# Four of sixteen token transposes move from TensorE to the DMA queues and VectorE

## What is computed

```python
xn = _layernorm(x)
# attention branch: 16 heads, decayed causal scores, layer norm, silu gate, wo
logits = xf @ router_w.T + router_b
top_vals, top_idx = jax.lax.top_k(logits, 4)
rw = softmax(top_vals) * 1.8
routed = sum over the 4 experts: rw * (silu(xf @ gate.T) * (xf @ up.T)) @ down.T
shared = silu(xf @ shared_gate.T) * (xf @ shared_up.T) @ shared_down.T
x = x + attention(xn) + routed + shared
```

## Time and profile before

| | |
|---|---|
| time, median of 3 runs (lowest to highest) | 200.17 us (200.09 to 200.4) |
| time of the profiled execution | 200.26 us |
| its span, first to last instruction | 198.4 us |
| granted TensorE clock | 1.0 of full speed |
| busy: PE, weight loads, DVE, ACT, POOL | 190.0, 142.7, 117.5, 96.7, 111.8 us |

### The profile page before, as it was taken

How to read it: one execution, slowest core, us unless ns; L and a number is a source line. 1 busy time by engine, 2 the same in 40 slices (tenths; PEclk the granted TensorE clock), 3 DMA queues, 4 the chain that set the end, 5 groups by cost and what they waited for, 6 DMA issues and landing times.

```text
span 198.4 us, 4872 instructions
## 1 busy us (share of the span) xinstructions
PE 190.0 (96%) x1734; PEld 142.7 (72%) x1734; DVE 117.5 (59%) x360; ACT 96.7 (49%) x242; POOL 111.8 (56%) x156
## 2 busy tenths in 40 slices
PE   8998999999998899899999999999999999999994
PEld 2665756778565667698888678887867877687863
DVE  3478789898897766765632532433342144426894
ACT  3146248555889342653238647734934941123500
POOL 4133057525979468777777677777877743730000
PEclk9999999999999999999999999999999999999999
DMA  4994999998000029999975634324433335229963
GB/s 133 316 374 159 332 403 421 446 444 378 7 0 3 5 56 380 384 358 366 366 288 149 223 106 140 97 90 138 123 104 98 115 91 220 79 82 292 373 262 132
DMA packets 15000, 42.33 MB, mean 213 GB/s; under 512 B 2677, under 2 KB 6138, under 8 KB 14336
## 3 DMA queue, kind: packets, MB, share of 16 engines
q1 hardware_dynamic: 11376, 33.03, 45.5%
q0 software_dynamic: 3456, 8.92, 13.3%
q10 hardware_dynamic: 144, 0.07, 0.2%
HBM read 34.66 MB, written 7.86 MB: 214 GB/s over the span
## 4 chain that ended last, share of the span: by engine, by line
PE 73%; DMA 7%; DVE 7%; issue 4%; POOL 4%; ACT 3%; SPq 0%; ACTq 0%; POOLq 0%; DVEq 0%
PE bank L1575 20%; PE bank L1591 8%; PE bank L1783 5%; PE bank L1589 5%; DMA xg_mem<-xn_rows,codes 4%; PE bank L1440 4%; PE bank L1450 3%; PE bank L1553 3%; DMA w_mem<-w_qkvg_dram 3%; PE bank L1541 3%; PE bank L1612 3%; PE bank L1515 3%; DVE w_mem L1105 2%; PE bank L1465 2%; PE bank L1817 2%
## 5 line engine op out<-in xcount | busy, mean ns | idle before, releaser
L1575 PE MATMUL bank<-xb_mem,w_mem 128*128 128x128 f32 x384 | 47.7, 276 | 0.1
L1575 PEld LDWEIGHTS bank<-xb_mem,w_mem 128*128 128x128 f32 x384 | 45.4, 192 | 0.8 <-issue 0.3
L838 POOL DMA_INDIRECT y_rows<-y_mem,codes x36 | 36.2, 1007 | 16.8 <-issue 9.4
L830 POOL DMA_INDIRECT xg_mem<-xn_rows,codes x36 | 35.4, 984 | 13.0 <-issue 9.7
L1160 DVE TENSOR_TENSOR h_mem<-h_mem,bank 128x128 f32<-128x128 f32 x32 | 9.2, 287 | 42.2 <-ACT h_mem L641 41.9
L1105 DVE TENSOR_TENSOR w_mem<-bank,w_mem 128x512 f32<-128x512 f32 x32 | 20.1, 682 | 2.9 <-PE bank L1465 2.8
L640 ACT ACTIVATE h_mem<-bank 128x128 f32<-128x128 f32 x32 | 8.9, 277 | 23.5 <-PE bank L1575 23.1
L1168 DVE COPY y_mem<-bank 128x256 f32<-128x256 f32 x36 | 15.0, 424 | 7.3 <-PE bank L1591 4.5
L653 ACT COPY w_mem<-w_mem 128x1024 f32 x16 | 16.0, 1042 | 3.2 <-PE bank L1630 2.2
L1591 PE MATMUL bank<-w_mem,h_mem 128*128 128x256 f32 x60 | 17.0, 405 | 0.0
L1440 PE MATMUL bank<-w_mem 128*128 128x128 f32 x128 | 15.9, 278 | 0.2 <-DMA w_mem<-w_qkvg_dram 0.2
(11 more groups left out here) (168 smaller groups left out, 320.7 us busy)
## 6 DMA issues: line engine op xcount, KB each, us to landing
w_mem<-w_exp_dram SPq DMA_DIRECT2D x3, 3456.0 KB, 21.6
w_mem<-w_late_dram SPq DMA_DIRECT2D x7, 1152.0 KB, 8.1
w_mem<-y_rows SPq DMA_DIRECT2D x8, 512.0 KB, 7.3
w_mem<-w_qkvg_dram SPq DMA_DIRECT2D x2, 512.0 KB, 6.3
w_mem<-decay_dram SPq DMA_DIRECT2D x2, 512.0 KB, 7.6
xn_rows<-w_mem SPq DMA_DIRECT2D x2, 512.0 KB, 3.4
xnt_rows<-w_mem SPq DMA_DIRECT2D x1, 1024.0 KB, 4.9
w_mem<-w_ovf_dram SPq DMA_DIRECT2D x16, 64.0 KB
```

What stands on the lines that cost most here:

```text
L830: nc.gpsimd.indirect_dma_start(xg[:, k % RING, :], None, xn_rows, bass.IndirectOffsetOnAxis(ap=codes[:, c, 0:1], axis=0),).then_inc(tok_in ...
L838: nc.gpsimd.indirect_dma_start(y_rows, bass.IndirectOffsetOnAxis(ap=codes[:, c, 1:2], axis=0), ysb[:, k % YRING, :], None, bounds_check=RO ...
L1575: last = nc.tensor.matmul(ps_gu[j][:, m * P:(m + 1) * P], w[:, o:o + P], xbT[:, p % 2, (2 * g + j) * P:(2 * g + j + 1) * P], start=(g == 0 ...
```

## The change

Blocks of the last four pairs (24 to 31; `FIRST = 12`) are transposed by DMA. The DMA transposes 2-byte elements, so the fp32 tokens are handled as two planes of 16-bit halves:

- In the head, ACT splits each of the eight tiles of `xn` into low halves and high halves (`split_tokens`) in `xg_mem`, four tiles at t = 1 and four at t = 2. SP stores them in device memory (`xn_halves`, 1 MB) ahead of the third batch of weights, and the writers of `pos_hot` on ACT and POOL wait for that store.
- For blocks 24 to 31, POOL gathers rows of `xn_halves`, SP issues a DMA transpose of the 128x512 block of 16-bit elements into a buffer `xp`, which lies in `ws_mem`, and DVE joins the planes into `xbT` (`take_tokens`). PE no longer transposes them and ACT no longer copies them.
- SP's order becomes: overflow groups 0 to 2, transposes of 24 to 27, overflow group 3, transposes of 28 to 31, then `ws_mem`, then `xnt_rows`. The load of `ws_mem` waits until DVE has joined all eight blocks.
- The semaphores `wo_in` and `tot_sb` become one each instead of one per block or tile, and PE waits for the loaded overflow weights in `down_overflow` instead of `gate_up_overflow`.

```diff
+FIRST = 12
-X_ORDER = [b for b in SEQ_X if b[0] == "O" or b[1] % 2 == 0]
+X_ORDER = [b for b in SEQ_X if b[0] == "O" or (b[1] % 2 == 0 and b[1] < 2 * FIRST)]
+        xg_halves = xg_mem[:, :].bitcast(U16).rearrange("p (a b) -> p a b", a=RING)
+        xn_staged = xg_mem[:, :].bitcast(U16).rearrange("p (t h d) -> p t h d", t=NT, h=2)
+        xn_split = xn.bitcast(U16).rearrange("p t (d h) -> p t h d", h=2)
+        xbT_halves = xb_mem[:, 0:4 * KT * P].bitcast(U16).rearrange("p (a g j n h) -> p a j h g n", a=2, g=KT, j=2, h=2)
+        xp = ws_mem[:, 0:4 * KT * P].bitcast(U16).rearrange("p (a j b n) -> p a j b n", a=2, j=2, n=P)
...
                 if p + BATCH_IN == EARLY:
+                    sp.wait_ge(st_halves, NT)
+                    sp.dma_start(xn_halves.rearrange("(p t) c -> p t c", p=P),
+                                 xn_staged.rearrange("p t h d -> p t (h d)")).then_inc(halves_out, 16)
                     sp.wait_ge(xnT_ps, len(HEAD))
...
-                if j == 0:
-                    sp.dma_start(ws_mem[:, :], w_shared).then_inc(ws_in, 16)
+            def transpose_block(n):
+
+                p, j, k = n // 2, n % 2, AT["P", n]
+                sp.wait_ge(tok_in[k % RING], 16 * (k // RING + 1))
+                if p >= FIRST + 2:
+                    sp.wait_ge(xt2_sb, 2 * (p - 2 - FIRST) + j + 1)
+                sp.dma_start_transpose(xp[:, p % 2, j], xg_halves[:, k % RING, :]).then_inc(tp_in[p % 2][j], 16)
+
+            for j in range(STATIC_O - 1):
+                group_in(j)
+            for n in range(2 * FIRST, 2 * FIRST + 4):
+                transpose_block(n)
+            group_in(STATIC_O - 1)
+            for n in range(2 * FIRST + 4, 2 * PAIRS):
+                transpose_block(n)
+            sp.wait_ge(xt2_sb, 2 * (PAIRS - FIRST))
+            sp.dma_start(ws_mem[:, :], w_shared).then_inc(ws_in, 16)
             sp.wait_ge(xt_ps, len(X_ORDER))
             sp.dma_start(xg_mem[:, :], xnt_rows).then_inc(xnt_in, 16)
...
+            def split_tokens(t):
+                act.wait_ge(xn_done, t + 1)
+                nc.scalar.copy(xn_staged[:, t], xn_split[:, t]).then_inc(st_halves, 1)
...
-                if 0 < s < PAIRS - 1:
+                if 0 < s < FIRST - 1:
                     take_pair_tokens(s + 1)
...
+            def take_tokens(n):
+
+                p, j = n // 2, n % 2
+                if j == 0:
+                    dve.wait_ge(gu_ps, 2 * (p - 1))
+                wait_transposed(dve, p, j)
+                nc.vector.tensor_copy(xbT_halves[:, p % 2, j], xp[:, p % 2, j].rearrange("p (h g) n -> p h g n", h=2)
+                                      ).then_inc(xt2_sb, 1)
...
             def expert_step(s):
                 if s < PAIRS:
                     multiply_unit(2 * s)
+                if FIRST <= s + 1 < PAIRS:
+                    take_tokens(2 * s + 2)
...
                 if 1 <= s and s != PAIRS - 1:
                     results(s - 1)
+                if FIRST <= s + 1 < PAIRS:
+                    take_tokens(2 * s + 3)
...
-                pe.wait_ge(xt_sb, X_AT["P", 2 * p] + 1)
+                if p < FIRST:
+                    pe.wait_ge(xt_sb, X_AT["P", 2 * p] + 1)
+                else:
+                    pe.wait_ge(xt2_sb, 2 * (p - FIRST) + j + 1)
...
-                if 0 < s < PAIRS - 1:
+                if 0 < s < FIRST - 1:
                     transpose_pair(s + 1)
```

More of the change, by code:

```diff
@@ L141, with build @@
 SENT = [sum(k % YRING == w for k in range(len(SEQ_Y))) for w in range(YRING)]
-X_ORDER = [b for b in SEQ_X if b[0] == "O" or b[1] % 2 == 0]
+X_ORDER = [b for b in SEQ_X if b[0] == "O" or (b[1] % 2 == 0 and b[1] < 2 * FIRST)]
 X_AT = {b: k for k, b in enumerate(X_ORDER)}
-def build(nc, x, consts, decay, w_router, w_qkvg, w_out, lnwb, rbias, w_exp, w_late, w_ovf2, w_shared, xn_rows, xnt_rows, y_rows, out):
+def build(nc, x, consts, decay, w_router, w_qkvg, w_out, lnwb, rbias, w_exp, w_late, w_ovf2, w_shared, xn_rows, xn_halves, xnt_rows, y_rows, out):
     with ExitStack() as ctx:
@@ L366, in build @@
         we_in = [sem(f"we_in{p}") for p in range(PAIRS)]
-        wo_in = [sem(f"wo_in{j}") for j in range(STATIC_O)]
+        wo_in = sem("wo_in")
         ones_sb = sem("ones_sb")
@@ L386, in build @@
         xt_sb = sem("xt_sb")
+        xt2_sb = sem("xt2_sb")
+        st_halves = sem("st_halves")
+        halves_out = sem("halves_out")
+        tp_in = [[sem(f"tp_in{a}{j}") for j in range(2)] for a in range(2)]
         gu_ps = sem("gu_ps")
@@ L418, in build @@
         diag_sb = sem("diag_sb")
-        tot_sb = [sem(f"tot_sb{i}") for i in range(NT - len(PE_TILES))]
+        tot_sb = sem("tot_sb")
         block = ctx.enter_context(nc.Block())
@@ L453, in down_bank, with whole_rows, wait_slot_read, wait_transposed @@
             return ps_dn[j][:, 0:D] if p < PAIRS - 1 else ps_sd[1][j][:, 0:D]
-        def x_done(k):
+        def whole_rows(k):
+            return SEQ_X[k][0] == "O" or SEQ_X[k][1] < 2 * FIRST
+        def wait_slot_read(eng, k):
             kind, n = SEQ_X[k]
-            return X_AT[kind, n - n % 2 if kind == "P" else n] + 1
+            if whole_rows(k):
+                eng.wait_ge(xt_ps, X_AT[kind, n - n % 2 if kind == "P" else n] + 1)
+            else:
+                wait_transposed(eng, n // 2, n % 2)
+        def wait_transposed(eng, p, j):
+            eng.wait_ge(tp_in[p % 2][j], 16 * ((p - FIRST) // 2 + 1))
         @block.sync
@@ L521, in _, with group_in @@
                     sp.wait_ge(y_ps, NT)
-                sp.wait_ge(we_in[p - 2 if p > EARLY else p - 1], 16)
-                late_pair_in(p)
-            for j in range(STATIC_O):
+                late_pair_in(sp, p)
+            def group_in(j):
                 experts = overflow_experts(SUBS * j)
                 if j == 0:
-                    sp.wait_ge(we_in[PAIRS - 1], 16)
                     sp.wait_ge(res_sb, NT)
@@ L551, in _ @@
                 else:
-                    sp.wait_ge(tot_sb[t], 1)
+                    sp.wait_ge(tot_sb, t + 1)
                 sp.dma_start(out_v[:, t, :], x_sb[:, t, :]).then_inc(out_done, 16)
@@ L710, in _ @@
                     take_features(3)
+                if t in (1, 2):
+                    split_tokens(4 * t - 4)
+                    split_tokens(4 * t - 3)
                 if t >= 2:
@@ L714, in _ @@
                 take_values_gate(t + 1)
+                if t in (1, 2):
+                    split_tokens(4 * t - 2)
+                    split_tokens(4 * t - 1)
                 hot_positions(t, "vg")
@@ L1317, in add_routed @@
                 if k == TOPK - 1 and n not in PE_TILES:
-                    ins.then_inc(tot_sb[n], 1)
+                    ins.then_inc(tot_sb, 1)
                 else:
@@ L1655, in down_overflow @@
                 pe.wait_ge(oht_sb, j + 1)
+                pe.wait_ge(wo_in, 16 * SUBS * (j + 1))
                 if j == 0:
@@ L1896 @@
     xn_rows = nc.dram_tensor("xn_rows", (TOK, D), F32, kind="Internal").ap()
+    xn_halves = nc.dram_tensor("xn_halves", (TOK, 2 * D), U16, kind="Internal").ap()
     xnt_rows = nc.dram_tensor("xnt_rows", (P, KT * TOK), F32, kind="Internal").ap()
     y_rows = nc.dram_tensor("y_rows", (ROWS, D), F32, kind="Internal").ap()
-    build(nc, *args, xn_rows, xnt_rows, y_rows, out)
+    build(nc, *args, xn_rows, xn_halves, xnt_rows, y_rows, out)
     r = run_bass_kernel_spmd(nc, [{n + "_dram": v for n, v in arrays.items()}], core_ids=[0])
```

19 lines of the change are left out of this document (12 added, 7 removed).

## The result

The changed kernel takes 203.06 us (median of 6 executions, 202.09 to 204.40), the kernel before beside it 200.25 (6 executions): a ratio of 1.0138 with a 95% interval of 1.0091 to 1.0185. It is slower by 2.8 us; 200.0 was predicted, and the range ended at 202.2.

The account below looks back on a forecast made before the run. PE was taken to bound the kernel. Terms -1.76 + 0.2 + 1.3 + 0.1, given as -0.17 on 200.26, made 200.1, less 0.09 for that execution lying over the median: 200.0 us, range 199.1 to 202.2.

Parts of the forecast that it names:

- PE's saving: Expert steps: four pairs' transposes leave PE, 0.44 us each on the chain, 1.76 us in all.
- the wait for the loads: Ahead of the shared expert: PE ready at 172.5, ws_mem and xnt_rows land at 173.8, so PE waits 1.3 us.
- the head: Start of the kernel: ACT's splits delay a copy PE needs; 0.1 us, bounds 0 and 0.3.
- the overflow weights: Step 13: ACT's copies of overflow block 3's weights end too late for PE; some 0.2 us lost.
- The four terms of the sum: Whole kernel: -1.76 PE's saving, +0.2 overflow weights, +1.3 wait for the loads, +0.1 head, given as -0.17 us.
- The transposes: DMA transposes of blocks 24 to 31: 4 us to landing, spacing up to 1.5, DVE waits 0.7 us, no cost.
- the two rules weighed: DMA transpose speed: one skill section gives 1309 ns per 128x128 square, the other says as fast as regular DMAs.
- late-halves rival: Head: store of halves lands at 48.3, holding ACT 1.7 us; up to 1.5 us more, 201.5; chance 0.10.
- The step that failed: Kernel's end: read-back from y_rows starts no later, its eight DMAs landing by about 192, nearly 4 us before the end.
- the rivals on record: Full gain, loads landing by 172.5 (198.7 us, chance 0.10); slow transposes (0.16); halves landing late (0.10).
- slow transposes: Blocks 28 to 31: DMA transposes hold each other up in one queue; 203.0 at 3.5 us spacing, chance 0.16.
- Every sign that was listed for the prediction being right: No line-1553 transposes after step 10; PE nearly gapless to 172.5, then 1.3 us gap ended by xnt_rows; ws_mem issued near 166.6.

Follow-up runs that it names:

- experiment 10: Kernel before plus only the head's splits, store of halves and waits on it, all transposes still on TensorE: 200.65 us, ratio 1.0013.
- Experiment 8: PE held before the shared expert by ACT copies. Kernel before: one 201.46 us, two 203.43, one plus late read-back 203.03; changed kernel without its two late loads: 200.93.
- experiment 6: Changed kernel, loads still late, with results of blocks 30 and 31 in memory of their own: 203.27 us, ratio 1.0146; profiled execution 200.67.
- experiment 3: Changed kernel with xnt_rows loaded once the last blocks in xg_mem are transposed, only ws_mem waiting for the last join: 199.57 us, ratio 0.9955.

## Why the prediction was wrong

**PE's saving and the wait for the loads** were right. PE is ready at 174.09 - 1.17 = 172.92 (172.5 forecast), `ws_mem` is issued at 166.78 (166.6), PE waits 1.17 us (1.3) and starts the shared expert where it did before (0.27 us earlier forecast). The 0.4 us of difference are 0.26 by which PE stood later at 139 us already, ahead of the first saved transposes (0.1 was put for the head; experiment 10 leaves 0 to 0.6), and 0.13 of PE's saving: the join of block 27 stood behind a copy that waited for a scatter, and PE lost 0.33 us there where 0.2 was put for the overflow weights. The four terms of the sum add up to -0.16, not -0.17.

**The transposes** were right, and better than their bounds: 3.3 us to landing where 4 was taken, 1.3 us apart, one wait of 0.8 on DVE where 0.7 was forecast, joins of 0.45 where 0.55 was. Of the two rules weighed, that of the Trainium skill in "VectorE: DVE Perf Modes", The three transpose paths, fell: its 1309 ns for each of four squares makes 5.2 us for a block, an estimate, and eight blocks landed in 3.1 to 3.8. They were not as fast as a plain transfer either: the 128 KB store took 1.8. The late-halves rival fell too: the store, issued at 38.78, needed 7.6 us by its line, to 46.4, and ACT's first write of `pos_hot` ran at 46.90 without a wait.

**The step that failed** is the sentence "The read-back from `y_rows` cannot start later for it: the last scatters follow `down_one`, which comes 1.5 us earlier, and its eight DMAs have landed by about 192, nearly 4 us before the end." Both halves are wrong. The last scatters follow `down_one` only if the slots of `y_mem` are free, and these come free when earlier scatters land; the moved load was put on top of just those scatters. The row for it was there: the copy at 167.46 that waited for a scatter in before, while `xnt_rows` was loading. I read it as a hold that the change takes away from step 13, and did not ask what the load would hold at its new place. And the slack of a transfer is not the time from the last landing to the end: the first additions stand ahead of `shared_hidden(3)` in DVE's list, so a read-back 1.85 us later moved the end by 0.7 in the kernel before, and one 1.66 us later by 1.3 in the changed kernel without loads.

**What was missing** is the clock. The prediction priced PE's wait at its length; in before no such pause exists there, and every term was taken from rows at full clock. Experiment 8 shows a pause of 1.49 us costing 3.1. The loss that the sum lacks has thus two parts: some 2.1 us in the executions at full clock (202.09 and 202.56 against 200.25), most of it by the late read-back (experiment 6 without it lost 0.4 at full clock), and some 1.4 more in the others. That a pause of PE is enough for the fall is shown by experiment 8, with and without the changed code; which of its two pauses it followed in the executions of the changed kernel that were not profiled is not known. Why pauses of like length were followed by a fall in some executions and not in others is open, as is the speed of the read-backs.

None of the rivals on record is what happened. The other side was given to slow transposes; the loss came from transfers that the change only moves. Every sign that was listed for the prediction being right was seen in the trace; none of them looked behind the start of the shared expert.

## What to carry to other kernels

When a transfer moves, list what else uses the DMA queues in the window that it moves into, and follow each of those to the buffer it frees and to the engine that waits for the buffer: a load that cost DVE 0.34 us at one place held a 128 KB scatter for 7 us at another, and DVE for 2.8. When a buffer is shared for a detour, as `ws_mem` was for the transposed halves, issue each load as soon as its own buffer is read for the last time: that alone, in experiment 3, turned +1.4% into -0.45%. A pause of an otherwise busy TensorE may cost twice its length, so a gap of a microsecond in the forecast deserves its own line in the sum and in the range.

## What the runs showed of the hardware

A scatter issued by POOL landed in 2.4 us when nothing else moved. In the changed kernel SP issued a 640 KB and a 1 MB load at 166.78 and 167.21, and three scatters issued at 167.18, 168.46 and 171.12 landed between 174.2 and 175.0 (after 7.06, 6.0 and 3.9 us), when the loads were through (174.0). With the 1 MB load cut into four, in shorter packets, scatters landed in 3.8 to 5.4 us, by the line of the scatters. The Trainium skill, "DMA: Bandwidth & Descriptors", Queues, rings and completion order, says that each DMA engine alternates between queue rows packet by packet. That shorter packets freed the scatters sooner goes with it; but packets and transfers were cut together, so no run here shows which of the two it was.

TensorE's granted clock fell to its 1.2 GHz level for a stretch of some 3 us after a pause of PE of 0.97 to 2.08 us, in some executions or in all, and after pauses of 0.84 to 1.27 us it stayed up in others. Executions with one such stretch took 1.4 us more in the changed kernel and 1.6 to 1.7 more in experiment 8, by the medians.
